# Splitting work between ScalarE, VectorE and GpSimd in a one-core kernel of two convolution blocks

## The reference, cut to what matters

```
x = x + conv0(group_norm(x))
x = x + relu(batch_norm(y) * gamma + beta),   y = conv_w . [g, up(cH), up(cV), up(cD)],  g = group_norm(x)
```

## Time and profile before

| what | value |
|---|---|
| median of three runs (lowest, highest) | 348.17 us (347.94, 349.41) |
| the profiled execution's own time | 347.7 us |
| its span | 346.0 us, so 1.7 us lie around the span |
| mean granted TensorE clock | 0.918 |
| busy: PE, DVE, ACT, POOL | 277.3, 286.3, 212.7, 222.1 us |
| chain of waits, by engine | DVE 41%, PE 22%, POOL 11%, DMA 8%, ACT 6%, issue 6% |

### The profile page before, as it was taken

One profiled execution on the slowest core, in us unless ns is written; L12 is line 12 of the kernel. 1 busy time (PEld: TensorE's weight loads), 2 busy tenths in 40 slices (PEclk: granted clock), 3 DMA queues, 4 the chain that ended last, 5 costly groups with the idle time before them and its releaser, 6 DMA issues.

```text
span 346.0 us, 4753 instructions
## 1 busy us (share of the span) xinstructions
PE 277.3 (80%) x1544; PEld 228.8 (66%) x1544; DVE 286.3 (83%) x528; ACT 212.7 (61%) x317; POOL 222.1 (64%) x211
## 2 busy tenths in 40 slices
PE   3565599999899979699999999999999998882000
PEld 0011189999788955677999998888999896751000
DVE  2799959988867736477789999999999999978892
ACT  0788736877776625545756767666666776340991
POOL 7487765592539997203888888888988888732000
PEclk9789869999999998899999999999999999986555
DMA  7999454579486286395000000000000000000599
GB/s 209 298 303 260 177 188 146 171 192 309 151 231 204 64 230 190 89 415 226 2 0 0 3 0 3 0 0 2 0 3 1 0 3 0 0 0 1 206 403 361
DMA packets 15064, 43.59 MB, mean 126 GB/s; under 512 B 2992, under 2 KB 3280, under 8 KB 15040
## 3 DMA queue, kind: packets, MB, share of 16 engines
q1 hardware_dynamic: 12736, 36.92, 32.8%
q10 hardware_dynamic: 1312, 4.20, 4.2%
q0 software_dynamic: 992, 2.19, 2.6%
HBM read 30.44 MB, written 8.39 MB: 112 GB/s over the span
## 4 chain that ended last, share of the span: by engine, by line
DVE 41%; PE 22%; POOL 11%; DMA 8%; ACT 6%; issue 6%; SPq 3%; DVEq 0%; POOLq 0%; ACTq 0%
PE wide L705 8%; DMA x_slot<-in_x 7%; DVE st L945 5%; DVE x_sb L1050 5%; DVE x_sb L938 4%; DVE y_sb L984 4%; DVE y_sb L977 3%; POOL d_split L406 3%; DVE sty L990 3%; POOL d_sb L296 3%; PE wide L241 2%; SPq L275 2%; DVE u_sb L921 2%; PE wide L243 2%; DVE u_sb L913 2%
## 5 line engine op out<-in xcount | busy, mean ns | idle before, releaser
L705 PE MATMUL wide<-t_all,s_hi 128*128 128x272 f32 (+1 forms) x320 | 47.0, 295 | 2.3 <-ACT t_all L512 1.2
L705 PEld LDWEIGHTS wide<-t_all,s_hi 128*128 128x128 f32 x320 | 43.0, 198 | 5.5 <-ACT t_all L512 2.9
L482 POOL TENSOR_TENSOR g_lo<-y_sb,g_hi 128x1024 fp32r<-128x1024 f32 x15 | 36.1, 2408 | 14.4 <-ACT y_sb L636 14.4
L458 POOL TENSOR_TENSOR g_lo<-y_sb,g_hi 128x1024 fp32r<-128x1024 f32 x15 | 36.0, 2400 | 13.2 <-ACT g_hi L609 13.2
L845 DVE TENSOR_TENSOR s_lo<-s_f,s_hi 128x768 fp32r<-128x768 f32 (+1 forms) x32 | 34.7, 1084 | 10.8 <-ACT s_hi L521 10.5
L635 ACT ACTIVATE g_hi<-x_sb,rs 128x1024 fp32r<-128x1024 f32 x16 | 21.4, 1336 | 34.1 <-POOL rs L467 34.1
L839 DVE STREAM_TRANSPOSE xa<-x_slot 128x1024 f32<-128x1024 f32 x16 | 31.1, 2010 | 8.6 <-DMA x_slot<-in_x 8.4
L241 PE MATMUL wide<-g_hi,t_hi 128*128 128x512 f32 x96 | 37.5, 391 | 0.7 <-DVE t_lo L965 0.7
L243 PE MATMUL wide<-g_hi,t_lo 128*128 128x512 f32 x96 | 37.5, 390 | 0.0
L242 PE MATMUL wide<-g_lo,t_hi 128*128 128x512 f32 x96 | 37.4, 389 | 0.0
L389 POOL TENSOR_TENSOR t_all<-t_f,t_all 128x512 fp32r<-128x512 f32 x17 | 26.3, 1556 | 10.7 <-ACT t_f L515 10.7
(11 more groups left out here) (130 smaller groups left out, 835.0 us busy)
## 6 DMA issues: line engine op xcount, KB each, us to landing
s_f<-in_taps SPq DMA_DIRECT2D x32, 384.0 KB, 4.4
x_sb<-in_x SPq DMA_DIRECT2D x8, 1024.0 KB, 9.4
out<-x_sb SPq DMA_DIRECT2D x7, 1024.0 KB, 5.1
x_slot<-in_x ACTq DMA_DIRECT2D x14, 256.0 KB, 13.7
x_slot<-in_x SPq DMA_DIRECT2D x14, 256.0 KB, 14.7
d_sb<-t_out SPq DMA_DIRECT2D x24, 76.5 KB, 2.9
d_sb<-t_out POOLq DMA_DIRECT2D x24, 76.5 KB, 4.7
out<-x_sb SPq DMA_DIRECT2D x2, 512.0 KB, 2.6
```

The source lines that it names most:

```text
L458: pool.tensor_tensor(g1_lo[:, W:W + HW], y_sb[:, n, :], g1_hi[:, W:W + HW].bitcast(F32), ALU.subtract).then_inc(s["g1_lo"], 1)
L482: pool.tensor_tensor(g2_lo[:, :], y_sb[:, n, :], g2_hi[:, :].bitcast(F32), ALU.subtract).then_inc(s["g2_lo"], 1)
L705: mm = pe.matmul(ps_t3[g % 2][:, j0 * NO:j1 * NO], weights[:, g % SR, 128 * t:128 * t + 128], t1_all[:, row + j0:row + j1, :].rearrange("p ...
```

## The change

Seven things are changed.

1. In the loop over g, ACT and VectorE do the taps of group g+2 after t3 of group g, in place of those of g+1 before it; group 1's taps are split before the loop. The side work of a turn comes after that.
2. d's pieces of blocks 0 and 1: ACT casts six (at g = 15, 18, 20, 22 and 25, 28), POOL two, and VectorE makes all eight low parts, inside the loop. POOL makes no low part of d.
3. POOL's program has its shuffles of block 1 together, and the shuffle of block 2 after the two casts. SP issues 7 of block 3's DMAs, POOL 9.
4. The turns at which SP issues the raw p5, the raw weights and the shuffles are moved (5 to 6, 18 to 21, 15 and 24 to 18 and 27), and ACT's turn for the weights from 18 to 16.
5. Images 2 and 3 are loaded by separate DMAs, as 0 and 1 were: four more DMAs.
6. `y_own` gives the sum of what it writes (`accum_out`), for each half of the rows. ACT takes the sum of squares of y(t-4) in one pass of 1024 elements between the evacuation of z and `g2_full_and_high`; the last image's in two passes. `y_statistics` goes.
7. `bn_aggr` is replaced by two reductions and three small operations.

```diff
-P5_RAW_AT = 5
-W_RAW_AT, W_DET_AT = 18, 18
-SHUFFLE_AT = (15, 24)
+P5_RAW_AT = 6
+W_RAW_AT, W_DET_AT = 21, 16
+SHUFFLE_AT = (18, 27)
-SP_BLOCKS, LAST_SP = 8, 9
-D_HI_AT = {15: 0, 17: 1, 19: 2, 21: 3}
+SP_BLOCKS, LAST_SP = 8, 7
+D_HI_AT = {15: (0, 0), 18: (0, 1), 20: (0, 2), 22: (0, 3), 25: (1, 0), 28: (1, 1)}
+D_HI_POOL = ((1, 2), (1, 3))
+D_LO_AT = {16: (0, 0), 19: (0, 1), 21: (0, 2), 23: (0, 3), 26: (1, 0), 27: (1, 2), 29: (1, 1), 30: (1, 3)}
...
@@ SP
-            for k in range(1, N // 2):
+            load_x(sp, x_slot[1][:, 0:1, :], 2, 3, x_in_third, (0, 1))
+            load_x(sp, x_slot[1][:, 1:2, :], 3, 4, x_in[1], (0, 1))
+            for k in range(2, N // 2):
...
@@ POOL
-            d_low(0, 0)
-            d_low(0, 1)
             d_ready(pool, 1)
             for i in range(2):
                 two_blocks(1, i)
-                d_low(0, 2 + i)
-            two_blocks(1, 2)
             pool.wait_ge(s["gst"], 1)
...
-            two_blocks(1, 3)
+            for i in range(2, 4):
+                two_blocks(1, i)
             w_forms()
-            wait_d(pool, 1)
-            for co in range(2):
-                d_high(co)
-                d_low(1, co)
+            for b, co in D_HI_POOL:
+                d_high(b, co)
             d_ready(pool, 2)
             shuffle(pool, 2, blocks[SP_BLOCKS:], d_in_pool[2])
-            for co in range(2, CI):
-                d_high(co)
-                d_low(1, co)
             d_ready(pool, 3)
             shuffle(pool, 3, blocks[LAST_SP:], d_in_pool[3])
...
@@ ACT
+            split_high(1)
             for g in range(G):
-                if g + 1 < G:
-                    split_high(g + 1)
                 act.wait_ge(s["conv"], g + 1)
...
                 if g >= 1:
                     t4_evacuate(g - 1)
+                if g + 2 < G:
+                    split_high(g + 2)
...
+            def y_square(n, parts):
+                act.wait_ge(s["y"], 2 * n + 2 - (parts - 1))
+                for a in range(parts):
+                    if parts > 1 and a:
+                        act.wait_ge(s["y"], 2 * n + 2)
...
+                    act.activation(junk, rows, ACT.Square, scale=1.0 / 128,
+                                   accum_out=y_squares[:, n, a:a + 1]).then_inc(s["y_sums"], 1)
...
                 if t >= 2:
                     z_evacuate(t - 2)
+                if t >= 4:
+                    y_square(t - 4, 1)
                 if 1 <= t <= N:
                     g2_full_and_high(t - 1)
...
+            y_square(N - 2, 1)
+            y_square(N - 1, 2)
...
@@ DVE, loop over g
-                if g + 1 < G:
-                    split_low(g + 1)
                 dve.wait_ge(s["t3_hi"], g + 1)
...
+                if g + 2 < G:
+                    split_low(g + 2)
...
+                if g in D_LO_AT:
+                    d_low(*D_LO_AT[g])
...
@@ DVE, y_own
                 for a in range(2):
-                    ins = dve.scalar_tensor_tensor(yr[:, a], zh[:, n % 2, 1:J + 1, :], 3.0, yr[:, a],
-                                                   ALU.mult, ALU.add)
-                ins.then_inc(s["y"], 1)
+                    dve.scalar_tensor_tensor(yr[:, a], zh[:, n % 2, 1:J + 1, :], 3.0, yr[:, a], ALU.mult, ALU.add,
+                                             accum_out=y_sums[:, n, a:a + 1]).then_inc(s["y"], 1)
...
@@ DVE, end
-            dve.wait_ge(s["sty"], 2 * N)
-            link(dve.bn_aggr(fin[:, 1:3], sty[:, :, :].rearrange("p n a -> p (n a)")))
+            link(dve.memset(y_squares[:, 0:N - 1, 1:2], 0.0))
+            dve.wait_ge(s["y"], 2 * N)
+            link(dve.tensor_reduce(fin[:, 1:2], y_sums, mybir.AxisListType.XY, ALU.add))
+            link(dve.tensor_scalar(fin[:, 1:2], fin[:, 1:2], 1.0 / (N * HW), None, ALU.mult))
+            dve.wait_ge(s["y_sums"], N + 1)
+            link(dve.tensor_reduce(fin[:, 2:3], y_squares, mybir.AxisListType.XY, ALU.add))
+            link(dve.tensor_scalar(fin[:, 2:3], fin[:, 1:2], fin[:, 1:2], fin[:, 2:3], ALU.mult, ALU.subtract))
+            link(dve.tensor_scalar(fin[:, 2:3], fin[:, 2:3], -1.0, None, ALU.mult))
```

More of the change, by code:

```diff
@@ L58 @@
 P5_AT, P5_LO_AT = 7, {9: 0, 10: 1, 11: 2, 12: 3}
-P5_RAW_AT = 5
-W_RAW_AT, W_DET_AT = 18, 18
-SHUFFLE_AT = (15, 24)
+P5_RAW_AT = 6
+W_RAW_AT, W_DET_AT = 21, 16
+SHUFFLE_AT = (18, 27)
 SHUFFLE_POOL_AT = 10
 PER_STEP = 2
-SP_BLOCKS, LAST_SP = 8, 9
-D_HI_AT = {15: 0, 17: 1, 19: 2, 21: 3}
+SP_BLOCKS, LAST_SP = 8, 7
+D_HI_AT = {15: (0, 0), 18: (0, 1), 20: (0, 2), 22: (0, 3), 25: (1, 0), 28: (1, 1)}
+D_HI_POOL = ((1, 2), (1, 3))
+D_LO_AT = {16: (0, 0), 19: (0, 1), 21: (0, 2), 23: (0, 3), 26: (1, 0), 27: (1, 2), 29: (1, 1), 30: (1, 3)}
+D_HI_ACT = list(D_HI_AT.values()) + [(b, piece) for b in (NB - 2, NB - 1) for piece in range(CI)]
 def build(nc, x, p1_blk_in, taps_in, p5_in, p6, w_in, gamma, beta, out):
@@ L188, in build @@
         g2_lo = put("g2_lo", [HW], F32R)
+        y_junk = put("y_junk", [HW])
         assert cursor[0] <= at_d
@@ L505, in _ @@
             load_x(act, x_slot[0][:, 1:2, :], 1, 2, x_in[0], (2, 3))
-            for k in range(1, N // 2):
+            load_x(act, x_slot[1][:, 0:1, :], 2, 3, x_in_third, (2, 3))
+            load_x(act, x_slot[1][:, 1:2, :], 3, 4, x_in[1], (2, 3))
+            for k in range(2, N // 2):
                 load_x(act, x_slot[k][:, :, :], 2 * k, 2 * k + 2, x_in[k], (2, 3))
```

57 lines of the change are left out of this document (27 added, 30 removed).

## The result

The changed kernel takes 338.75 us (median of 4 runs, 337.9 to 340.01) against 348.23 us for the kernel before (4 runs, 347.94 to 349.41): ratio 0.9724, 95% interval 0.9682 to 0.9767. The forecast was 336.7, range 332.5 to 342.3. The profiled execution took 337.9 us, with a span of 336.1 (before: 347.7 and 346.0).

A forecast was written before the change was run, and what follows sets the result against it. DMA was taken to bound the first stage, stalls to add 8.8 us in the convolution stage, PE and VectorE to be level in the loop. 347.7 - 4.9 (convolution) - 5.3 (between stages) - 0.3 (loop) - 0.5 (end) = 336.7 us; range 332.5 to 342.3.

The forecast's parts named there:

- Taps order: Convolution stage: side work behind the taps removes 5.4 us of d-cast stalls and about 1.5 of 3.4 us other stalls.
- Low parts of d on VectorE: Convolution stage: eight pieces of 1.36 us fit tightly on VectorE, at 2.0 us of new stalls; stage 4.9 us saved.
- the upper bound of 5.6: Convolution stage: most new stalls allowed, every low part of d late by a whole ACT cast, 8 x 0.7 us.
- the signs of being wrong: Loop turn below 9.4 or above 9.8 us; PE waiting for taps' low parts; casts of d waiting for block 1 shuffles.
- Rival 3: Convolution stage: VectorE is full and its low parts give back what the order gains; 341.6 us, chance 0.10.
- Between the stages: From the last t4 copy to the transposes: t5 starts 3.6 us earlier, kept clock saves 1.8; 5.3 us taken.
- Image loop: PE and VectorE level; with y's statistics off VectorE, PE keeps 9.6 to 9.67 us a turn; 0.3 us saved.
- Rival 1: Image loop: VectorE alone is the bound, so the turn falls by 0.9 us; 325.3 us, chance 0.08.
- Rival 2: Image loop: the accumulating form of y_own runs at half rate, costing 2 x 0.6 us more; 342.2 us, chance 0.08.
- rival 4: Image loop: sums in y_own cost more than the 10.7 us all other parts save, so slower; chance 0.04.
- End: After the loop: two statistics and the aggregation become half a square pass, two reductions and small operations; 0.5 us saved.
- Start: Loading images 2 and 3 apart gains nothing, as the last x load's landing covers it; without that cover up to 1.7 us.

The follow-up runs named there:

- the feeds mended: Changed kernel with GpSimd's taps for 10 groups, shuffles at 15 and 24, weights at 18, GpSimd's block 1 pairs ahead of the power: 333.49 us, ratio 0.9578.
- the run with more products: Changed kernel with four more matmuls of 256 columns in each turn of the image loop: 345.34 us, ratio 0.9923.

## Why the prediction was right, and where it was wrong

The direction was right and for a good part the reasons too. That the total came within 2.1 us is luck, because misses of opposite sign nearly cancel: the conv stage came out 6.3 us worse than forecast, the start, the gap and the loop 2.2, 2.2 and 0.9 better.

*Taps order.* "5.4 us and about 1.5 of the 3.4 fall away": they did, but only the second for the reason given. The statistics passes: the steps of groups 4 and 7 take 2.73 us each under the old order and 1.90 and 1.91 under the new, 1.65 together. Of the 1.36 us of a cast of d, 0.1 to 0.3 went with the order, and the rest with GpSimd's low part of d, which had stretched VectorE's. The working saw that row ("its low part at 86.08 for 1.93 us is beside a taps' low part of 2.08") and set it against the new stalls without a size. The 6.9 us measured by undoing the order agree with 5.4 + 1.5 by luck: they are for the most part waits for late shuffles, which the kernel before did not have, and the clock behind them. There the order does help, since the taps no longer stand behind a cast that waits.

*Low parts of d on VectorE.* "I take 2.0 us of new stalls for the stage" is the step that failed; if 6.9 fell away and the stage still grew by 1.4, they were 8.3, outside the upper bound of 5.6. The bound counted VectorE's work and a late cast, and neither is what was short: with the feeds mended, VectorE does the same low parts and the stage takes 71.84, 4.8 less than before (that 4.9 was forecast is a coincidence, as the parts differ). The missing terms are three feeds and the clock. The shuffles were asked for three groups later (part 4 of the change, which the working gave no price; casts waiting for shuffles stood only among the signs of being wrong). GpSimd still read taps beside VectorE in groups 10 to 13, though the working said that with its low parts of d gone it "no longer reads beside VectorE", and the new order put the low parts of p5 beside these reads. Small needed things (raw weights, group statistics) stood behind large ones. And a stall was priced at its own length, where the stall at group 13 was followed by a stretch at the lower clock that cost 1.5 us more. These terms don't add up: each hides the next, so that mending one gave nothing that the medians could tell, and the edits together 5.3 us (338.75 to 333.49). How much of it the weights and GpSimd's order are worth alone was not measured.

*Rival 3, VectorE full in the convolution stage*, is refuted by the same run, although the stage did what this rival said: VectorE was busy 62.19 of 71.84 us and the stage was still 6.2 us shorter than in the changed kernel.

*Between the stages.* The -5.3 was -7.5. "Add 4.14 for landing": the transfer took 2.04, because x pair 1 now goes out at 130.74, after GpSimd's last shuffle at 130.47, and no longer while it is under way; the run that put it back measured 4.67. "The unread products end ... 11.2 after the mark": they ended at 7.9 + 125.69 - 126.31 = 7.3, because image pair 0 was asked for at 119.86, 6.4 us ahead of the mark (before 121.67 and 126.60, 4.9), and landed 5.0 us later (before 6.4), so PE had no pause and ran them at the full clock. In three other runs this landing took 7.1 to 7.6 us, and there PE was the late one, as forecast. "So t5 starts at 11.2": 8.0. "1.8 saved" by the clock kept: 9.34 against 8.15 is 1.2, as the first matmuls are paced by the pieces of d.

*Image loop.* -0.3 was taken and -1.2 found, inside the bounds "0 and 1.2"; the turn fell from 9.681 to 9.62, which is 0.8 over 13 turns. PE as the bound was right. Rival 1 is refuted by the turn itself, which fell by 0.06 and not 0.9, and by the run with more products. Rival 2 is refuted by the trace: `y_own` takes 704 ns and not 682, and successive ones start 0.61 us apart. The rule of the Trainium skill (Vector Engine (DVE) Microarchitecture Reference, Points that are easy to get wrong) would have made that 1.2 us; for this form, two float32 sources in SBUF, the measurement decides against it. With it rival 4 falls, which needed 1.6 us. The accumulator's reading, put at 0.15 us, took 0.08 and ran beside the next instruction. VectorE's 8.47 was the turn less 1.2; its busy time of 9.48 less 1.2 would be 8.28, and 8.88 was measured, 0.7 under PE. ScalarE's pass fits where it was put: its wait for the norm factors fell by 1.09 us to 1.12.

*End.* -0.5 forecast, -0.4 measured. *Start:* 0 was taken, with "up to 1.7 us" named beside it; the third transpose's wait of 1.73 us fell away, and what that gave is left open.

## What to carry to other kernels

A moved issue (a shuffle three turns later, a weight load) needs a price like a moved instruction: for each consumer, compare the turn at which it would ask with issue plus landing, since an engine made faster arrives earlier at a transfer that does not. Where several waits stand in one stage, the first hides the others; removing one at a time may show nothing, and a run that removes all of them together shows what they are worth. A run that undoes an edit measures it in the company of the others: read from the steps of the trace which stalls came back before calling the sum confirmed. A stall of PE can cost more than its length, if the granted clock falls behind it. And what a large load does to a small transfer on the critical path was set here by which of them was issued first.
